# Key and row score products of a low-rank attention as side-by-side pairs of 64-row matmuls

## The reference, cut to what matters

```python
c_q  = h_t @ W_DQ + b_DQ                 # 32 dims
c_kv = h_t @ W_DKV + b_DKV               # 32 dims
q = concat(c_q @ W_UQ + b_UQ, c_q @ W_QR + b_QR)       # per head 128 + 32 dims
k = concat(c_kv @ W_UK + b_UK, h_t @ W_KR + b_KR)
scores = q @ k.T / sqrt(160)
o = softmax(scores) @ (c_kv @ W_UV + b_UV)
out = o @ W_O + b_O
```

## Time and profile before

| | |
|---|---|
| time, median of 3 runs | 1807.89 us (1807.46 to 1809.03) |
| span of the profiled execution | 1812.5 us |
| TensorE busy | 1670.4 us (92%) |
| VectorE busy | 1393.8 us (77%) |
| GpSimd busy | 1177.3 us (65%) |
| ScalarE busy | 1137.5 us (63%) |
| first key score product to last | 610.8 to 1777.7 us |

### The profile page before, as it was taken

How to read it: one execution, slowest core, us unless ns; L and a number is a source line. 1 busy time by engine, 2 the same in 40 slices (tenths; PEclk the granted TensorE clock), 3 DMA queues, 4 the chain that set the end, 5 groups by cost and what they waited for, 6 DMA issues and landing times.

```text
span 1812.5 us, 39662 instructions
## 1 busy us (share of the span) xinstructions
PE 1670.4 (92%) x15057; PEld 1223.0 (67%) x15057; DVE 1393.8 (77%) x2976; ACT 1137.5 (63%) x2222; POOL 1177.3 (65%) x909
## 2 busy tenths in 40 slices
PE   4679999999877899999999999999999999999995
PEld 4557777777766567666766766766676677677674
DVE  5557777766597888878888888888887888888862
ACT  5447777777676466666666666666656666665662
POOL 4300111000066498898898988989889898898892
PEclk9889999999887899999999999999999999999997
DMA  4556666654000000000000000001001000100101
GB/s 123 136 140 156 162 156 159 164 136 116 29 1 1 1 10 8 10 8 10 7 13 16 10 8 19 11 7 22 7 10 19 8 10 7 22 7 10 19 10 30
DMA packets 198677, 81.47 MB, mean 45 GB/s; under 512 B 152553, under 2 KB 177493, under 8 KB 198357
## 3 DMA queue, kind: packets, MB, share of 16 engines
q1 hardware_dynamic: 198484, 78.93, 19.5%
HBM read 39.79 MB, written 29.88 MB: 38 GB/s over the span
## 4 chain that ended last, share of the span: by engine, by line
PE 54%; DVE 11%; POOL 2%; issue 1%; ACT 1%; DMA 0%; SPq 0%; POOLq 0%; ACTq 0%
PE pair L1825 12%; PE pair L1878 11%; PE pair L1882 11%; PE pair L1936 10%; DVE amax L1833 4%; PE pair L1929 4%; PE pair L1650 2%; DVE o_inv L1946 1%; PE pair L1641 1%; DVE stats L485 1%; POOL w_mix L1907 1%; PE pair L1664 1%; DVE q_low L1754 1%; DVE cq L1765 1%; DVE key_hl L1768 1%
## 5 line engine op out<-in xcount | busy, mean ns | idle before, releaser
L1893 ACT ACTIVATE prob<-pair 128x512 f32<-128x512 f32 x1024 | 604.4, 597 | 422.2 <-PE pair L1882 359.6
L1833 DVE TENSOR_REDUCE amax<-pair 128x1 f32<-128x512 f32 x1024 | 670.3, 682 | 133.9 <-PE pair L1825 131.8
L1825 PE MATMUL pair<-key_hl,q_hi 128*128 128x512 f32 x1024 | 437.8, 430 | 11.2 <-DVE amax L1833 7.1
L1878 PE MATMUL pair<-q_hi,key_hl 128*128 128x512 f32 x1024 | 405.2, 396 | 2.6 <-ACT prob L1893 2.6
L1882 PE MATMUL pair<-q_low,key_h 65*128 65x512 f32 x1024 | 406.0, 396 | 0.0
L1907 POOL TENSOR_TENSOR w_mix<-w_mix,prob 128x1024 f32<-128x1024 f32 x160 | 382.3, 2389 | 25.2 <-ACT prob L1893 8.5
L1907 POOL TENSOR_TENSOR Wm<-Wm,prob 128x1024 f32<-128x1024 f32 x155 | 369.6, 2384 | 20.8 <-ACT prob L1893 4.1
L520 POOL TENSOR_SCALAR veps<-mv 128x8 f32<-128x8 f32 x47 | 11.4, 243 | 452.6 <-DVE mv L493 451.2
L1825 PEld LDWEIGHTS pair<-key_hl,q_hi 128*128 128x128 f32 x1024 | 196.1, 192 | 115.9 <-issue 51.0
L1936 PE MATMUL pair<-prob,values 128*32 128x256 f32 x4096 | 247.2, 382 | 0.0
L1186 DVE TENSOR_REDUCE mx_neg<-pair 128x4 f32<-128x512 f32 x256 | 164.9, 687 | 94.8 <-PE pair L1090 94.1
(11 more groups left out here) (209 smaller groups left out, 2232.8 us busy)
## 6 DMA issues: line engine op xcount, KB each, us to landing
rows_mem<-once SPq DMA_DIRECT2D x128, 128.0 KB, 2.0
queries<-rows_mem SPq DMA_DIRECT2D x64, 256.0 KB, 4.5
keys<-rows_mem SPq DMA_DIRECT2D x16, 1024.0 KB, 7.1
rows_mem<-once SPq DMA_DIRECT2D x128, 64.0 KB, 1.9
q_low<-shift_cols SPq DMA_DIRECT2D x512, 0.5 KB, 2.0
yT<-o_norm SPq DMA_DIRECT2D x256, 32.0 KB, 1.9
x<-x_dram SPq DMA_DIRECT2D x8, 512.0 KB, 7.3
out_dram<-x SPq DMA_DIRECT2D x7, 512.0 KB, 3.4
```

The lines of the kernel that those rows point to most:

```text
L1825: e.matmul(row_bank(("row", r, i)), q_hi[:, k, t * P:(t + 1) * P], key_hl[:, b % 2, i * HALF:(i + 1) * HALF], start=True, stop=True, skip_ ...
L1833: e.tensor_reduce(amax1[:, u % 2, t, i:i + 1], row_bank(("row", r, i)), AX_X, ALU.max).then_inc(*row_maxed.up((r, i)))
L1878: e.matmul(bank(j), key_hl[:, b % 2, ks], q_hi[:, k, sl], start=True, stop=False, skip_group_check=True)
L1893: e.activation(prob1[:, g % P_BUFS, half * HALF:(half + 1) * HALF], bank(K_BANKS[(2 * g + half) % 3]), ACT.Exp, scale=SCALE1).then_inc(*ke ...
```

## The change

The keys are stored as two tiles, `key_high` and `key_low`, each with its 64 rows twice (partitions 0 to 63 and 64 to 127). The queries are stored so that the first 512 queries lie in partitions 0 to 63 and the last 512 in 64 to 127, with 512 columns each: `q_hi`, `q_low`, and a tile of its own for the shift, `q_shift` (row 0 and row 64, the rest zero). Row scores become one pair of 64-row matmuls a step, one query tile of either half against 512 keys, with the high keys alone. Key scores become four pairs a step: high keys x high queries, low keys x high queries, high keys x low queries, and `ones_shift` x `q_shift`. A unit has one query item with two accumulating products instead of two items. The key pair of a step waits for both of its banks before its first matmul. Items are begun only at steps 3 and 7 of a unit, at step 3 also one behind the weighing (`after`).

```diff
-            if u % NH == t == half == 0:
-                e.wait_ge(*key_h1_done.at((b, 1)))
-            if n >= 3:
-                e.wait_ge(*key_exp.at(divmod(n - 3, 2)))
-            e.matmul(bank(j), key_hl[:, b % 2, ks], q_hi[:, k, sl], start=True, stop=False, skip_group_check=True)
-            if t == 0:
-                e.wait_ge(*q_lo_done.at((u, half)))
-                e.wait_ge(*shift_ready(u, half))
-            e.matmul(bank(j), key_h1[:, b % 2, ks], q_low[:, k, sl], start=False, stop=True,
-                     skip_group_check=True).then_inc(*key_scored.up((g, half)))
+            banks = [bank(K_BANKS[(2 * g + side) % 3]) for side in range(2)]
+            for side in range(2):
+                if 2 * g + side >= 3:
+                    e.wait_ge(*key_exp.at(divmod(2 * g + side - 3, 2)))
+            for part in range(4):
+                if t == 0 and part == 2:
+                    e.wait_ge(*q_lo_done.at((u, 0)))
+                if t == 0 and part == 3:
+                    e.wait_ge(*shift_ready(u))
+                for side in range(2):
+                    rows = slice(side * KR, (side + 1) * KR)
+                    weights = ones_shift[rows, :] if part == 3 else (key_low if part == 1 else key_high)[rows, b % 2, ks]
+                    moving = (q_hi, q_hi, q_low, q_shift)[part][rows, k, :]
+                    ins = e.matmul(banks[side], weights, moving, start=part == 0, stop=part == 3, skip_group_check=True)
+                    if part == 3:
+                        ins.then_inc(*key_scored.up((g, side)))
...
-            e.matmul(row_bank(("row", r, i)), q_hi[:, k, t * P:(t + 1) * P], key_hl[:, b % 2, i * HALF:(i + 1) * HALF],
-                     start=True, stop=True, skip_group_check=True).then_inc(*row_scored.up((r, i)))
+            for side in range(2):
+                row_bank_free(e, ("row", r, side))
+            for side in range(2):
+                rows = slice(side * KR, (side + 1) * KR)
+                e.matmul(row_bank(("row", r, side)), q_hi[rows, k, t * P:(t + 1) * P],
+                         key_high[rows, b % 2, half * HALF:(half + 1) * HALF], start=True, stop=True,
+                         skip_group_check=True).then_inc(*row_scored.up((r, side)))
...
-                e.matmul(bank(j), w_query[:, h, :], cq[:, b % 2, sl], start=True, stop=True,
+                e.matmul(bank(j), w_query[:, h, KR:3 * KR], cq[:, b % 2, 0:HALF], start=True, stop=False,
+                         skip_group_check=True)
+                e.matmul(bank(j), w_query[:, h, 0:2 * KR], cq[:, b % 2, HALF:T], start=False, stop=True,
                          skip_group_check=True).then_inc(*query_done.up((a, i)))
...
-                    ins = e.matmul(bank(j)[:, t * DC:(t + 1) * DC], key_hl[:, a % 2, t * P:(t + 1) * P], both_parts[:, :],
-                                   start=True, stop=True, skip_group_check=True)
+                    for part in (key_high, key_low):
+                        ins = e.matmul(bank(j)[:, t * DC:(t + 1) * DC], part[:, a % 2, t * P:(t + 1) * P],
+                                       first_dims[:, :], start=part is key_high, stop=part is key_low,
+                                       skip_group_check=True)
...
-                e.tensor_tensor(q_low[0:KR, a % Q_BUFS, sl], bank(j)[0:KR, :], q_hi[0:KR, a % Q_BUFS, sl],
-                                ALU.subtract).then_inc(*q_lo_done.up((a, i)))
+                e.tensor_tensor(q_low[:, a % Q_BUFS, :], bank(j), q_hi[:, a % Q_BUFS, :], ALU.subtract).then_inc(
+                    *q_lo_done.up((a, i)))
...
-                e.scalar_tensor_tensor(out=key_hl[KR:P, k, sl], in0=bank(j)[0:KR, :], scalar=b_low[0:KR],
-                                       in1=key_hl[0:KR, k, sl].bitcast(F32), op0=ALU.add, op1=ALU.subtract).then_inc(
-                    *keys_done.up((a, i)))
+                for rows in (slice(0, KR), slice(KR, P)):
+                    ins = e.scalar_tensor_tensor(out=key_low[rows, k, sl], in0=bank(j)[0:KR, :], scalar=b_low[0:KR],
+                                                 in1=key_high[0:KR, k, sl].bitcast(F32), op0=ALU.add, op1=ALU.subtract)
+                ins.then_inc(*keys_done.up((a, i)))
...
-                    e.memset(key_h1[KR:KR + 1, :, :].bitcast(F32), 1.0).then_inc(*set_low.up("key row"))
+                    e.memset(ones_shift[:, :].bitcast(F32), 1.0)
+                    e.memset(q_shift[:, :, :].bitcast(F32), 0.0).then_inc(*set_low.up("shift rows"))
...
-        if item is None and waiting and (g % 2 == 0 or g >= NT * U):
+        if item is None and waiting and (g % NT == 3 or g >= NT * U):
             item = waiting.pop(0)
...
+        if g % NT == 3 and 0 <= g < NT * U and waiting and item[0] != "low" and waiting[0][0] != "low":
+            run = begin(waiting.pop(0))
+            after.append((tuple(run[:3]), 1))
```

More of the change, by code:

```diff
@@ L251, in regular @@
     def regular(g):
-        for i in range(2):
-            u, rest = divmod(g + 16 - 4 * i, NT)
-            if rest == 0 and 0 <= u < U:
-                return "query", u, i
-        return None
+        u, rest = divmod(g + PIPELINE, NT)
+        return ("query", u, 0) if rest == 0 and 0 <= u < U else None
     opening = {"bias": [((("bias", 0, 0), None, None), 1)]}
@@ L1801, in build_program @@
         row_uses = []
-        for g, early, late in plan_m:
+        for g, early, late, after in plan_m:
             if 0 <= g + ROW_LEAD < total:
@@ L2013, in pe_low_rank @@
                     pe_weigh(e, g // 4 - 1)
+                for (item, j, before), part in after:
+                    pe_low_part(e, item, j, before, part)
         def act_low_rank(e):
-            for g, early, late in plan_m:
+            for g, early, late, after in plan_m:
                 if g == LAST_C["copy"]:
```

180 lines of the change are left out of this document (91 added, 89 removed).

## The result

| | before | changed |
|---|---|---|
| median (lowest to highest), us | 1808.46 (1807.46 to 1812.22) | 2054.09 (2044.62 to 2057.38) |
| ratio of the times | | 1.133, 95% interval 1.129 to 1.137 |
| span of the profiled execution, us | 1812.5 | 2051.6 |
| first to last key product, us | 610.8 to 1777.7: 1167 | 624.8 to 2017.1: 1392 |

The change makes the kernel 246 us slower. The forecast was 1983 us, 175 slower, with 1935 to 2055 as its range. The median lies 0.9 us inside that range, and one of the four executions (2057.38 us) lies outside it.

A forecast was written before the change was run, and what follows sets the result against it. PE's own work was taken to bound the loop. Exposed waits 162 + 3, items 15 and other waits (39 - 44) made 175 us: span 1812.5 to 1987, less 4.6, 1983 us; range 1935 to 2055, 8 in 10.

The forecast's parts named there:

- The mechanism: Loop, six of eight steps: key pair waits for ACT's exponential, a turn of 0.95 us; 162 us over 64 units.
- A pair costs one pass: Loop, PE: two 64-row matmuls run side by side in 0.233 us, saving 1.86 us of PE a unit.
- Rival 2: Loop, PE: pairs don't run side by side; 418 us in all, 2400 us; chance 5%.
- rival 1: Loop: the wait for the exponential is hidden and the passes are saved; 95 us less, 1713 us; chance 4%.
- Rival 3, the clock: Loop, PE: granted clock falls to 1.2 GHz for half of 384 cycles; 165 us on top, 2148 us; chance 9%.
- cycle: Loop, from one key pair's stream to the next, without a weighing between: 1.88 us, with PE streaming for 1.17.
- other excess in these 384 steps: Loop, step 6 of a unit: ACT scales four tiles ahead of an exponential; 1.6 us a batch, 11 over seven.
- the 127 steps with a weighing: Loop, transitions at steps 3 and 7 of a unit: a weighing of 2.07 us or more covers the turn.
- 0.04 back: Loop, part of the turn: PE starts 0.04 us after ACT's exponential ends.
- A memset reads nothing, so I take 0: Ahead of the loop: POOL's new memset of 1536 columns costs 0, bounded above by 3.6 us.
- The row scores ahead of the loop go at DVE's pace and stay: Stretch before the loop: row scores are paced by DVE, so their time doesn't change.
- Waits of DVE and POOL: Loop: both have over 25 us more room a batch, so edits cost nothing; 12 us added for DVE's small groups.

## Why the forecast was right or wrong, by its steps

**The mechanism: right.** The forecast said that the key pair would wait for the first exponential of the step before, in six of eight steps of a unit, with PE and ACT waiting for each other at the full clock. The timeline shows this, and one more bank for the key scores takes it away. (That this saved 163 us and that the forecast's term is 162 is chance: the term is what the turn costs less what the passes save. What can be compared is a unit without items, 19.71 us where the forecast had 19.18.)

**A pair costs one pass: right.** Pairs are 0.23 us apart. Rival 2 is out. So is rival 1: the key pairs wait; the hidden turn exists only in the versions with four banks or lagged sides, at 1.34 to 1.43 us a cycle, where the forecast had put the point of no loss at 1.42. For a unit without items that point is about right (16.75 us with four banks and a cycle of 1.40 to 1.41, 16.65 before). The kernel as a whole is 50 us slower even so: 40 of them are the loop (1206 us, 1167 before), and since 64 x 0.10 = 6, nearly all of that lies in the units with items; the rest is the longer start (below) and the spread of executions.

**Rival 3, the clock: not in this kernel,** with 0.98 to 1.00 in the windows of the loop (36 of 1392 us at 1.2 GHz), but it comes with the next 0.42 us of idle time.

**Where the 71 us come from.** The loop took 1392 us, not 1341; it started 14 us later; the tail is the same (34.5 and 34.8 us); and the median lies 2.5 us above the profiled span, where the forecast carried over 4.6 below: 51 + 14 + 7 = 72.

| term | forecast | measured | difference, us |
|---|---|---|---|
| cycle, x384 | 1.88 | 1.94 | +23 |
| other excess in these 384 steps | 11 (at step 6) | (1.994 - 1.94) x 384 = 21 | +10 |
| the 127 steps with a weighing | 1341 - 722 - 11 = 608 | 625.8 | +18 |
| start of the loop | 610.8 | 624.8 | +14 |
| median less span | -4.6 | +2.5 | +7 |

Of these 72 us some 11 belong to no term of the sum: the last line, and 3.9 of the 14 (below), differ from execution to execution. The other 60 are real and all of one sign, so that the median still fell inside the range is owed to its width upwards, not to the sum.

*The cycle.* The term that was too small is "0.04 back". The 0.04 came from a key product of before, with one unmet wait; the changed code puts two waits ahead of its pair, and the load starts 0.11 us after the exponential's end. The row of before was right for its own code, not for the new one; leaving the met wait out gave the 0.04 again. That a met wait costs 0.06 us each time was in no row that I had read.

*Steps with a weighing.* Some 12 us are the step with the query between the weighing and the row pair, 3.99 us where the forecast's terms give 2.07 + 5 x 0.233 + 0.47 + 0.10 = 3.80, and 63 x 0.19 = 12: PE changes its shape twice there, and I priced one change. The items are 15.7 us a batch. The forecast's rows give 14.1, and with the 12 us that it added for DVE's groups 15.8, so their size was right, and the other 6 us of this line I can't place. What the forecast missed about the items is a choice: it asked what they cost at their new place and not what they had hidden at the old one. At the old places they would have stood in the turns, and the kernel would have been some 107 us faster.

*The start of the loop, 14 us.* Of these 3.9 were there at the end of the first stage, which the change doesn't touch: the last product of that stage's scores starts at 456.7 us before and at 460.6 after. In the profiles of the ten other versions, in all of which this stage is the same, it lies between 450.5 and 455.9 us. This part is the spread between executions, not a cost. "A memset reads nothing, so I take 0" stands, within the 0.9 us of its experiment. "The row scores ahead of the loop go at DVE's pace and stay" is wrong, by 10 us: from the last group of quantised products ahead of the row scores to the first key product it took 36.1 us before (574.68 to 610.8) and takes 46.3 after (578.47 to 624.8), and 46.3 also in the versions with one wait, with the sides one after the other, and with the late memset. Two rows of the timeline of the changed kernel:

```profile
578.47 1.40 PE L1321 MATMUL pair<-cst,prob 128*128 128x128 f32 x8 [2.09 <-POOL prob L1261]
...
615.75 0.79 PE L1843 MATMUL pair<-key_high,q_hi 64*128 64x512 f32 x2 [0.84 <-DVE amax L1852]
```

A row pair needs two of three banks as well: here one comes every 1.64 us, with PE idle for about half of the time, while DVE's two maxima take 1.29. And the whole stretch ran at 1.2 GHz, where before part of it had the full clock. How much of the 10 us is this turn and how much the clock stays open.

*Waits of DVE and POOL.* The forecast said that such waits would show its accounting of room as wrong. The list of waits in the loop (640 to 2000 us) names DVE too:

```profile
PEld pair L1906 <- ACT prob L1918: 258.0, 330, 1.5
PEld pair L1843 <- DVE amax L1852: 68.0, 114, 2.0
```

The 68 us are 114 waits of a row pair; the other waits of weight loads for DVE are under 10 us each. Here is the one at the low product: PE's and DVE's timelines of the changed kernel.

```profile
1222.77 0.75 DVE L1774 SCALAR_TENSOR_TENSOR cq<-pair,Wt,cq 32x512 fp32r<-32x512 f32 x1
...
1223.12 0.50 PE L1906 MATMUL pair<-q_hi,key_high 64*128 64x512 f32 x2 [0.33 <-ACT prob L1918]
...
1223.55 1.50 DVE L1778 SCALAR_TENSOR_TENSOR key_low<-pair,Wt,key_high 64x512 fp32r<-64x512 f32 x2
...
1225.08 1.29 DVE L1852 TENSOR_REDUCE amax<-pair 128x1 f32<-128x512 f32 x2
...
1225.92 0.50 PE L1843 MATMUL pair<-key_high,q_hi 64*128 64x512 f32 x2 [1.62 <-DVE amax L1852]
```

Three operations of 0.75 us stand ahead of two maxima, and the row pair waits 1.62 us. With 1.88 - 1.36 = 0.52 us of room a cycle a group of 2.25 us can't be hidden. The forecast had counted room over a batch, where there was enough, and added 12 us for these groups: less than these waits sum to, though the total of the steps with a weighing came near; how much of the 68 us stands in the place of a wait for an exponential I haven't separated.

## What to carry to other kernels

Two half-height matmuls side by side cost one pass (0.23 us here), but two banks fall due at once: with three banks, count how long the consumer of one bank takes from the last matmul's end to its own (0.16 + 0.04 + 0.60 + 0.04 us here) against the work that stands between, not the consumer's throughput. Give each side its own wait and issue one side behind the other: the halves run beside each other anyway and each asks for its bank as late as it can. Where a turn stays exposed, put small independent work into it, and leave out waits that another one implies.

## What the runs showed of the hardware that I had not expected

- Matmuls of the two 64-row halves start independently of program order between them: 1209.84 us for a side issued behind one whose third product started at 1209.87.
- A second wait, already met, ahead of a pair: 0.11 us instead of 0.05 from the exponential's end to the weight load (medians 0.114 and 0.051), 17 us of the loop.
- A wait that comes 0.42 us later cost 249 us instead of 163, since the granted clock fell from 0.99 and 1.00 to between 0.86 and 0.94 in windows of the loop; 326 us of it ran at 1.2 GHz instead of 36.
- PE's busy share reached 98% (157.19 of 160 us) in a version that is 4% slower than before: with lagged halves it counts time in which half of the array stands still.
- The first stage, the same in all twelve kernels, ended up to 10 us apart in their profiles (450.5 to 460.6 us at the start of its last score product). A shift of this size ahead of the stage that an edit touches says nothing of the edit.
